# One core, five stages: attention's second scores of four heads in one block, routers with one exponential per step, counts in four pieces and list work shared anew

## The chip, the core and the metric

The kernel runs on one core of a Trainium2 chip. Its time is the device time of one execution in microseconds (us). The core has TensorE (PE; its weight loads are listed as PEld), VectorE (DVE), ScalarE (ACT), GpSimd (POOL) and the queue engine SyncE (SP). SP, ACT and POOL can issue DMAs; 16 DMA engines carry them. Engines run side by side, each in its own program order, and wait for one another through semaphores.

## The reference, cut to what matters

The program is two layers on 4096 tokens (16 sequences of 256) of 256 numbers. Two of its parts are touched by the change.

```python
def _moe(x, gate_w, w_gate, w_up, w_down):
    logits = x2 @ gate_w.T
    probs = jax.nn.softmax(logits.astype(jnp.float32), axis=-1)
    top_w, top_i = jax.lax.top_k(probs, K)
    ...
    pos = jnp.sum(jnp.cumsum(onehot, axis=0) * onehot, axis=-1) - 1
    valid = pos < C
```

There are E = 64 experts, K = 8 for each token and C = 128 places in each expert. The mixture of experts runs twice. Its first half, the router, gives each token's softmax weights and, for each expert, the list of its first 128 tokens in token order.

```python
def _chunk_abc(q, k, v, s):
    z = jax.lax.cumlogsumexp(s, axis=2)
    ...
    _, okT = jax.lax.scan(step_k, hk0, (qT, kT, pT, gT))
    pvT = jax.nn.softmax(okT, axis=-1)
    ...
    _, ovT = jax.lax.scan(step_v, hv0, (pvT, vT, pT, gT))
```

The attention has 16 heads and 64 slots and runs once, between the two mixtures. In the kernel both recurrences are causal products of 256 x 256 per head: the first scores are k times q, the second are exp(s) times pz (the softmax over slots divided by the running sum of exp(s)).

## The kernel before, in words

The stages follow one another, each in a block of its own: router 1 (`moe_router`, tiles `r_`), experts 1 (`e_`), attention (`a_`), router 2, experts 2, closing (`f_`). The order of each engine is written out by hand.

**Router.** NJ = 8 steps `j` of four tiles of 128 tokens: tiles 2j and 2j+1 of the lower half of the tokens and the same two of the upper half. Per step: DVE takes moments (`moments_of(j + 2)`), POOL makes `rstd` and `shift`, ACT normalises into `row` (L289), PE turns `row` (L474), ACT copies to `lnT` (L298), PE scores against the gate (L484), DVE copies logits, finds the eight largest, the negative maximum `nm` (L395), and the chosen experts (`choose(j)`). ACT then takes four exponentials, one per tile, with their sums (L319), DVE the reciprocal, and ACT scales the four into `row` (L327, four instructions). PE turns the chosen mask (L502) and DVE runs a cumulative count over the half (`cum`, L418). After step 6 (`EARLY`) ACT writes the counts of the first 12 tiles of each half to DRAM, after step 7 the rest (L304). They come back into `local` with tile number on the partitions (L218): 8 DMAs for the early part, 8 for the rest. Then comes the list work. PE sums the counts of earlier tiles (L507), DVE and POOL add them to `local`, half each (L430, L368), DVE marks which tile holds each slot (`reached` L433, `holds` L438), PE picks that tile's counts in 24 groups (L518) into six banks, and each group is counted in turn by DVE (even groups, L448) or ACT (odd groups, `Sign`, L342). The result, `slot_tok` (L462), is what the experts gather by.

**Attention.** N = 64 units `n` of four heads of one sequence. PE has a fixed order in which projections of unit n+1 (fp32r, `split_matmul`, L1432 to L1434) stand between the products of unit n. The second scores, `scores_b`, use two banks `psB`, one per head; heads are 64 rows deep (L1250, L1251), even heads on rows 0 to 63 and odd on 64 to 127. DVE masks each into `at` (L1081, `masked`). Because there are two banks, heads 0 and 1 go first, then `gate(n + 1, 0)`, then heads 2 and 3, then `gate(n + 1, 1)`, then `over_j`. `psD` (two banks) holds the turned output of unit n-1 until DVE has taken the low part of it (`low_of_output`, L1061, semaphore `otl_ok`), and then the result of `over_j(n)`.

Of the kernel before, what the change touches and what calls it, by code (L numbers as in the profile page):

```python
# [6 lines left out]

# [9 lines left out]
ALU = mybir.AluOpType  # L17
# [120 lines left out]
def moe_router(nc, cst, tag, past, x_src, gate_w, rows, fresh, slot_tok, counts):  # L138
# [6 lines left out]
    EARLY = 6  # L145
# [3 lines left out]
    with ExitStack() as ctx:  # L149
# [15 lines left out]
        nm = mem.sb("nm", [P, 2, 4])  # L165
        left = mem.sb("left", [P, 2, 2, E])
        chosen = mem.sb("chosen", [P, 2, 2, E])
        ex = mem.sb("ex", [P, 2, 2, 2, E])
# [24 lines left out]
        top, nm_ok, exps, rden_ok, weights = (mem.sem(n) for n in ("top", "nm_ok", "exps", "rden_ok", "weights"))  # L193
# [3 lines left out]
        cum_out = mem.sem2("cum_out")  # L197
# [3 lines left out]
        by_half = counts.rearrange("(e h r) -> h e r", h=2, r=HALF * P)  # L201
        by_tile = counts.rearrange("(g f h r t) -> f h r g t", f=4, h=2, r=HALF, t=P)
# [11 lines left out]
        def count_back(engine, parts, r0, r1):  # L214

            for f, h in parts:
                at = 32 * f + HALF * h
                engine.dma_start(local[at + r0:at + r1, :, 0:P], by_tile[f, h, r0:r1]).then_inc(local_here, 16)  # L218

        xv = x_src.rearrange("(h j p) d -> j p h d", h=2, p=P)  # L220
        rv = rows[0:NTOK, :].rearrange("(h j p) d -> j p h d", h=2, p=P)
        if fresh:
            stream_a, stream_b = fresh
            av = stream_a[0:NTOK, :].rearrange("(h j p) d -> j p h d", h=2, p=P)
            zv = stream_b.rearrange("(p k r) d -> p k (r d)", p=P, k=NZ)
        QUARTERS = [(f, h) for f in range(4) for h in range(2)]

        with nc.Block(no_gpsimd_drain=True) as block:  # L228
            @block.sync
            def _(sp):  # L230
# [14 lines left out]
                def rows_written(j):  # L245
                    sp.wait_ge(weights, 4 * j + 4)
                    for u in range(2):
                        sp.dma_start(rv[2 * j + u], row[:, j % R, u, :, :]).then_inc(row_out[j % R], 16)
# [5 lines left out]
                if fresh:  # L254
# [3 lines left out]
                    for k in range(NZ):  # L258
                        sp.dma_start(zv[:, k, :], zeros[:, :]).then_inc(zero_out, 16)
                for j in range(NJ - 1):  # L260
# [8 lines left out]
                rows_written(NJ - 1)  # L269
                sp.wait_ge(cum_out[1], 32)  # L270
                count_back(sp, QUARTERS[0:4], 2 * EARLY, HALF)
                if fresh:
                    for j in range(NJ - R, NJ):
# [8 lines left out]
            def _(act):  # L282
# [17 lines left out]
                def counts_out(r0, r1):  # L300
                    for u in range(2):
                        act.wait_ge(keyed[u], r1 // 2)
                    for h in range(2):
                        act.dma_start(by_half[h][:, r0 * P:r1 * P], cum[h * E:(h + 1) * E, r0 * P:r1 * P]).then_inc(cum_out[r0 > 0], 16)  # L304

# [5 lines left out]
                for j in range(NJ):  # L311
                    if j + 1 < NJ:
                        turned_out(j + 1)
                    act.wait_ge(nm_ok, j + 1)
                    if j >= 2:
                        act.wait_ge(weights, 4 * (j - 1))
                    for u in range(2):
                        for h in range(2):
                            nc.scalar.activation(ex[:, j % 2, u, h, :], lg[:, j % 2, u, h, :], ACT.Exp,  # L319
                                                 bias=nm[:, j % 2, 2 * u + h:2 * u + h + 1],  # L320
                                                 accum_out=den[:, j % 2, 2 * u + h:2 * u + h + 1]).then_inc(exps, 1)
                    if j + 2 < NJ:
                        normalise(j + 2)
                    act.wait_ge(rden_ok, j + 1)
                    for u in range(2):
                        for h in range(2):
                            nc.scalar.activation(row[:, j % R, u, h, D:ROW], ex[:, j % 2, u, h, :], ACT.Copy,  # L327
# [1724 lines left out]
```

## Time and profile before

| what | us |
|---|---|
| median of 3 runs (lowest, highest) | 2782.9 (2782.44, 2787.22) |
| the profiled execution's own time | 2797.33 |
| its span, first to last instruction | 2795.6 |
| PE busy | 2432.8 (87%) |
| DVE busy | 1789.0 (64%) |
| ACT busy | 888.8 (32%) |
| POOL busy | 1238.2 (44%) |

A view by windows gives busy time of each engine in a stretch, the TensorE clock that was granted (1.00 is 2.4 GHz, 0.50 is 1.2 GHz), the busy share of the 16 DMA engines and what they moved. Router 1 lies between 7 and 117 us of the span, experts 1 until about 375, attention until 1907, router 2 until 2018, experts 2 until about 2240, and the closing stage takes the rest.

### The profile page before, as it was taken

What the parts mean: (1) busy time and instruction counts of PE and PEld (TensorE: products, weight loads), DVE (VectorE), ACT (ScalarE), POOL (GpSimd) and SP (SyncE); (2) the same over time, 40 slices, a digit from 0 to 9 for tenths busy, and PEclk for the clock granted to TensorE, in tenths of its full rate; (3) what the DMA queues carried; (4) which work ended last, traced back from release to release, by engine and by line L of the source; (5) the groups of instructions that cost most, each with busy time, mean ns of one, the idle gap of its engine ahead of it and who ended that gap; (6) DMA issues with size and microseconds to landing.
All of it is one profiled execution on the core that took longest, in us unless ns stands there. A gap on an engine that the chain in (4) does not pass through costs nothing. (4 is left out here: it accounts for less than half of the span.)

```text
span 2795.6 us, 44639 instructions
## 1 busy us (share of the span) xinstructions
PE 2432.8 (87%) x16926; PEld 2117.8 (76%) x16926; DVE 1789.0 (64%) x3524; ACT 888.8 (32%) x1886; POOL 1238.2 (44%) x1200
## 2 busy tenths in 40 slices
PE   6465669999999999999999999996466578999997
PEld 5354458888888888888888888885455457888886
DVE  5332348877887787777777777774422247767654
ACT  6322223333333333333333333324422123333332
POOL 2277725454555455545544554542168712222110
PEclk9578889999999999999999999995588889999999
DMA  6698810000000000000000000003499710000000
GB/s 217 173 257 214 191 31 5 16 20 10 15 16 20 5 20 16 20 5 20 16 20 5 17 19 20 5 8 94 108 271 217 165 55 18 29 23 24 9 16 16
DMA packets 193219, 169.53 MB, mean 61 GB/s; under 512 B 28816, under 2 KB 185456, under 8 KB 192496
## 3 DMA queue, kind: packets, MB, share of 16 engines
q1 hardware_dynamic: 163776, 117.12, 14.2%
q0 software_dynamic: 24576, 37.77, 7.3%
q10 hardware_dynamic: 4656, 11.80, 1.4%
q8 instruction: 137, 2.24, 0.3%
q14 instruction: 74, 0.61, 0.1%
HBM read 117.94 MB, written 53.13 MB: 61 GB/s over the span
## 5 line engine op out<-in xcount | busy, mean ns | idle before, releaser
L1081 DVE TENSOR_TENSOR a_at<-a_psB,causal 128x384 f32<-128x384 f32 x512 | 260.6, 550 | 115.3 <-PE a_psB L1251 115.2
L948 POOL TENSOR_TENSOR a_orstd<-a_ms,minus_half 128x8 f32<-128x8 f32 x64 | 106.7, 1668 | 511.3 <-DVE a_ms L1108 510.0
L928 POOL TENSOR_SCALAR a_pick<-a_index,lut_row 128x258 f32<-128x258 int32 x240 | 279.9, 1166 | 24.3
L1101 DVE RECIPROCAL a_rz<-a_rz 128x256 f32<-128x256 f32 x128 | 215.6, 1716 | 0.0
L635 PE MATMUL e_psX<-ident,e_xg 128*128 128x128 f32 x256 | 64.5, 341 | 164.6 <-DMA e_xg<-rows,slot_tok 164.4
L759 DVE TENSOR_TENSOR e_hT<-e_psH,e_sil 128x128 f32<-128x128 f32 x128 | 37.3, 291 | 261.6 <-ACT e_sil L716 261.6
L635 PEld LDWEIGHTS e_psX<-ident,e_xg 128*128 128x128 f32 x256 | 33.3, 164 | 209.0 <-DMA e_xg<-rows,slot_tok 203.8
L931 POOL TENSOR_TENSOR a_found<-a_found,a_pick 128x258 f32<-128x258 f32 x240 | 177.5, 739 | 20.1
L1312 PEld LDWEIGHTS a_psD<-a_v,a_at 128*128 128x128 f32 x1536 | 181.3, 192 | 5.6
L1312 PE MATMUL a_psD<-a_v,a_at 128*128 128x128 f32 x1536 | 181.9, 275 | 0.0
L605 POOL DMA_INDIRECT e_xg<-rows,slot_tok x128 | 128.9, 1007 | 81.5 <-POOLq L228 43.1
L959 ACT ACTIVATE a_v<-a_psA 128x512 f32<-128x512 f32 x128 | 76.6, 598 | 246.6 <-PE a_psA L1434 246.6
L1432 PE MATMUL a_psC<-wo_high,a_oT 128*128 128x256 f32 x512 | 151.7, 296 | 1.5 <-DVE a_oT L1061 1.5
L1432 PE MATMUL f_pair<-f_lnT,wguT 128*128 128x512 f32 (+1 forms) x352 | 143.1, 406 | 7.5 <-DVE f_lnT L1698 7.2
L1433 PE MATMUL a_psC<-wo_low,a_oT 128*128 128x256 f32 x512 | 144.5, 282 | 0.0
L1434 PE MATMUL a_psC<-wo_high,a_oT 128*128 128x256 f32 x512 | 144.3, 282 | 0.0
L1433 PE MATMUL f_pair<-f_lnT,wguT 128*128 128x512 f32 (+1 forms) x352 | 140.4, 399 | 0.0
L1434 PE MATMUL f_pair<-f_lnT,wguT 128*128 128x512 f32 (+1 forms) x352 | 140.2, 398 | 0.0
L1709 DVE TENSOR_TENSOR f_hs<-f_pair,f_sil 128x512 f32<-128x512 f32 x96 | 66.1, 689 | 115.7 <-PE f_pair L1434 105.6
L953 POOL TENSOR_TENSOR a_o<-a_o,a_orstd 128x512 f32<-128x512 f32 x128 | 130.9, 1044 | 5.0
L1031 ACT ACTIVATE a_sq<-a_psD 128x512 f32<-128x512 f32 x128 | 76.5, 598 | 171.6 <-PE a_psD L1312 127.2
L959 ACT ACTIVATE a_emT<-a_psC 128x512 f32<-128x512 f32 x64 | 38.2, 597 | 283.5 <-DVE a_rz L1097 283.5
(248 smaller groups left out, 7532.0 us busy)
## 6 DMA issues: line engine op xcount, KB each, us to landing
e_wg<-in_L_ffn_w_gate SPq DMA_DIRECT2D x128, 128.0 KB, 3.5
e_wu<-in_L_ffn_w_up SPq DMA_DIRECT2D x128, 128.0 KB, 3.8
e_wd<-in_L_ffn_w_down SPq DMA_DIRECT2D x128, 128.0 KB, 4.3
rows<-r_row SPq DMA_DIRECT2D x32, 320.0 KB, 3.2
stream_b<-r_zeros SPq DMA_DIRECT2D x11, 384.0 KB, 6.0
stream_c<-rows SPq DMA_DIRECT2D x33, 128.0 KB, 3.2
r_xt<-in_L_attn_hidden_states SPq DMA_DIRECT2D x16, 256.0 KB, 3.9
stream_a<-r_xt SPq DMA_DIRECT2D x16, 256.0 KB, 5.2
```

The lines of the kernel that those rows point to most:

```text
L605: pool.indirect_dma_start(out=xg[:, e % U, :], out_offset=None, in_=rows, in_offset=bass.IndirectOffsetOnAxis(ap=slot_tok[:, e:e + 1], axi ...
L928: nc.gpsimd.tensor_scalar(pick[:, :, :], index[:, :, :], float(c), w["lut"][:, c:c + 1], ALU.is_equal, ALU.mult).then_inc(picked, 1)
L931: nc.gpsimd.tensor_tensor(out=found[:, :, :], in0=found[:, :, :], in1=pick[:, :, :], op=ALU.add).then_inc(looked, 1)
L948: nc.gpsimd.tensor_tensor(out=flat(orstd[:, :, :]), in0=ms[:, :], in1=cst["minus_half"][:, 0:TT * HQ], op=ALU.pow).then_inc(orstd_ok, 1)
L953: nc.gpsimd.tensor_tensor(out=part, in0=part, in1=orstd[:, :, 2 * a:2 * a + 2].unsqueeze(3).to_broadcast([P, TT, 2, DV]), op=ALU.mult).the ...
L959: nc.scalar.activation(out, in_, ACT.Copy, scale=scale).then_inc(done, 1)
L1081: nc.vector.tensor_tensor(out=at[:, h, :], in0=psB[h % 2][:, 0:3 * P], in1=cst["causal"][:, :, :].rearrange("p a i -> p (a i)"), op=ALU.mu ...
L1101: nc.vector.reciprocal(rz[:, a, :], rz[:, a, :]).then_inc(rz_ok, 1)
L1312: mm = nc.tensor.matmul(psD[:, t, h * DV:(h + 1) * DV], bt[:, h, i * P:(i + 1) * P], v[:, n % 2, j, h * DV:(h + 1) * DV], start=(j == 0), ...
L1432: nc.tensor.matmul(out, lhs[0], rhs[0], start=first, stop=False)
L1433: nc.tensor.matmul(out, lhs[0], rhs[1], start=False, stop=False)
L1434: return nc.tensor.matmul(out, lhs[1], rhs[0], start=False, stop=last)
```

## The change

The second scores of all four heads are issued in one block, heads 2 and 3 into the banks of `psD`; `over_j` waits for all four masks at once. In the routers, a step covers four tiles that follow one another in token order; DVE subtracts the maximum from all four tiles in one instruction (`below`), ACT takes one exponential of 256, DVE sums and inverts it, and POOL scales it into `row` (`weigh`). The counts go out in four pieces, three issued by SP in the course of the steps, and come back in four. In the list work ACT adds the counts of earlier tiles (16 instructions) and takes 9 of the 24 groups; DVE takes 15. In router 1, six of the eleven zero writes stand behind the counts' return on SP.

```diff
-        xv = x_src.rearrange("(h j p) d -> j p h d", h=2, p=P)
+        xv = x_src.rearrange("(j h p) d -> j p h d", h=2, p=P)
-        by_half = counts.rearrange("(e h r) -> h e r", h=2, r=HALF * P)
+        by_half = counts.rearrange("(e r h t) -> h e r t", r=HALF, h=2, t=P)
...
+        def by_sign(k):
+            return k % 4 == 3 or (k % 4 == 1 and k // 4 < len(TRIPLES) // 2)
+        def counts_out(engine, piece):
+            for u in range(2):
+                engine.wait_ge(keyed[u], STEP // 2 * (piece + 1))
+            r = slice(STEP * piece, STEP * (piece + 1))
+            for h in range(2):
+                engine.dma_start(by_half[h][:, r, :], cum[h * E:(h + 1) * E, r.start * P:r.stop * P].rearrange("e (r t) -> e r t", t=P)
+                                 ).then_inc(cum_out[piece], 16)
+        def count_back(engine, piece, quarters):
+            engine.wait_ge(cum_out[piece], 32)
+            k = slice(2 * STEP * piece, 2 * STEP * (piece + 1))
+            for f in quarters:
+                engine.dma_start(local[32 * f + k.start:32 * f + k.stop, :, 0:P], by_tile[f, k]).then_inc(local_here, 16)
...
-                    if j == EARLY:
-                        sp.wait_ge(cum_out[0], 32)
-                        count_back(sp, QUARTERS, 0, 2 * EARLY)
+                    piece, second = divmod(j, 2)
+                    if second and piece < NP - 1:
+                        counts_out(sp, piece)
+                    if not second and piece > 0:
+                        count_back(sp, piece - 1, range(4))
+                count_back(sp, NP - 1, (0, 1))
...
-                            nc.scalar.activation(ex[:, j % 2, u, h, :], lg[:, j % 2, u, h, :], ACT.Exp,
+                    nc.scalar.activation(ex[:, j % 2, :, :], below[:, j % 2, :, :], ACT.Exp).then_inc(exps, 1)
...
-                            nc.scalar.activation(row[:, j % R, u, h, D:ROW], ex[:, j % 2, u, h, :], ACT.Copy,
...
+                counts_out(act, NP - 1)
+                count_back(act, NP - 1, (2, 3))
+                act.wait_ge(passed_ok, 1)
+                act.wait_ge(local_here, 16 * 4 * NP)
+                for g in range(NG):
+                    nc.scalar.activation(local[:, g, 0:P], local[:, g, 0:P], ACT.Identity, bias=local[:, g, P + 1:P + 2]).then_inc(spread, 1)
...
-                    nc.vector.tensor_scalar(nm[:, j % 2, :], mx[:, j % 2, :, 0], -1.0, None, ALU.mult).then_inc(nm_ok, 1)
+                    nc.vector.tensor_tensor(out=below[:, j % 2, :, :], in0=lg[:, j % 2, :, :, :].rearrange("p u h e -> p (u h) e"),
+                                            in1=mx[:, j % 2, :, 0].unsqueeze(2).to_broadcast([P, 4, E]), op=ALU.subtract).then_inc(below_ok, 1)
...
+                    nc.vector.reduce_sum(den[:, j % 2, :], ex[:, j % 2, :, :], axis=AX.X).then_inc(den_ok, 1)
...
+                def weigh(j):
+                    pool.wait_ge(rden_ok, j + 1)
+                    nc.gpsimd.tensor_tensor(out=row[:, j % R, :, :, :].rearrange("p u h c -> p (u h) c")[:, :, D:ROW], in0=ex[:, j % 2, :, :],
+                                            in1=rden[:, j % 2, :].unsqueeze(2).to_broadcast([P, 4, E]), op=ALU.mult).then_inc(weights, 1)
...
-                def scores_b(n, heads):
+                def scores_b(n):
                     pe.wait_ge(pzt_ok, n + 1)
                     pe.wait_ge(et_ok, n + 1)
-                    for h in heads:
+                    for h in range(HQ):
                         if h < 2:
                             pe.wait_ge(at_ok, HQ * n + h + 3)
-                        else:
-                            pe.wait_ge(bt_ok, HQ * n + h - 1)
-                        causal_scores(emT, pzT, h, bt_ps)
+                        elif n > 0:
+                            pe.wait_ge(otl_ok, NH * n)
+                        causal_scores(emT, pzT, h, bt_ps, psO)
```

On PE, the place in attention is a unit in which `turn_stream` also stands; `psB0`, `psB1` and `psD` are banks, `wg` the gate's weights. Before:

```order
L1250 MATMUL a_psB0<-a_pzT,a_emT 128x256
L1251 MATMUL a_psB0<-a_pzT,a_emT 128x128
L1250 MATMUL a_psB1<-a_pzT,a_emT 128x256
L1251 MATMUL a_psB1<-a_pzT,a_emT 128x128
L1432 MATMUL a_psA0<-wg_high,a_lnT 128x512
...
L1187 MATMUL a_psC0<-ident,a_xab 128x128 x4
L1250 MATMUL a_psB0<-a_pzT,a_emT 128x256
L1251 MATMUL a_psB0<-a_pzT,a_emT 128x128
L1250 MATMUL a_psB1<-a_pzT,a_emT 128x256
L1251 MATMUL a_psB1<-a_pzT,a_emT 128x128
L1432 MATMUL a_psA1<-wg_high,a_lnT 128x512
```

The same place in the changed kernel (L1268 and L1269 are the former L1250 and L1251, L1449 the former L1432):

```order
L1268 MATMUL a_psB0<-a_pzT,a_emT 128x256
L1269 MATMUL a_psB0<-a_pzT,a_emT 128x128
L1268 MATMUL a_psB1<-a_pzT,a_emT 128x256
L1269 MATMUL a_psB1<-a_pzT,a_emT 128x128
L1268 MATMUL a_psD<-a_pzT,a_emT 128x256
L1269 MATMUL a_psD<-a_pzT,a_emT 128x128
L1268 MATMUL a_psD<-a_pzT,a_emT 128x256
L1269 MATMUL a_psD<-a_pzT,a_emT 128x128
L1449 MATMUL a_psA0<-wg_high,a_lnT 128x512
...
L1204 MATMUL a_psC0<-ident,a_xab 128x128 x4
L1449 MATMUL a_psA1<-wg_high,a_lnT 128x512
```

The four score instructions of heads 2 and 3 moved ahead of the first half of the gate; the number of instructions is the same.

On SP, router 1 from the last load of `r_xt` to the end of the router. Before:

```order
L238 DMA r_xt<-in_L_attn_hidden_states 128x2x256 x2
L248 DMA rows<-r_row 128x2x320 x6
L218 DMA r_local<-counts 12x16x128 x8
L248 DMA rows<-r_row 128x2x320 x2
L218 DMA r_local<-counts 4x16x128 x4
L243 DMA stream_a<-r_xt 128x2x256 x8
```

The changed kernel, the same stretch (L230 writes counts, L238 now reads them back, L293 writes zeros):

```order
L257 DMA r_xt<-in_L_attn_hidden_states 128x2x256 x2
L230 DMA counts<-r_cum 64x4x128 x2
L267 DMA rows<-r_row 128x2x320 x2
L238 DMA r_local<-counts 8x16x128 x4
L267 DMA rows<-r_row 128x2x320 x2
L230 DMA counts<-r_cum 64x4x128 x2
L267 DMA rows<-r_row 128x2x320 x2
L238 DMA r_local<-counts 8x16x128 x4
L267 DMA rows<-r_row 128x2x320 x2
L238 DMA r_local<-counts 8x16x128 x2
L293 DMA stream_b<-r_zeros 128x768 x6
L262 DMA stream_a<-r_xt 128x2x256 x8
```

Behind the last `rows` only two reads are left on SP (and two on ACT), where there were 8 ahead of it and 4 behind it.

## Rows read from the trace of the kernel before

**Rows 1.** The page's first line

```profile
span 2795.6 us, 44639 instructions
```

**Rows 2.** Windows: length, busy time (x instructions) of PE, PEld, DVE, ACT, POOL, clock, DMA, GB/s

```profile
387.00:1890.00 1503.00, 1496.69 (x11712) 1317.48 (x11713) 1186.88 (x1884) 481.16 (x836) 745.32 (x738) 1.00 0.05 14
1920.00:1976.60 56.60, 46.41 (x208) 39.57 (x208) 35.04 (x208) 41.97 (x142) 11.35 (x26) 0.53 0.39 121
1976.60:1994.20 17.60, 0.15 (x1) 0.15 (x1) 0.01 (x1) 0.49 (x3) 0.00 (x0) 0.50 0.70 153
```

**Rows 3.** Timeline of PE in router 1: start, us, engine, line

```profile
42.80 2.10 PE L474 MATMUL r_bank<-ident,r_row 128*128 128x128 f32 x8 [1.50 <-ACT r_row L289]
45.22 3.67 PE L484 MATMUL r_bank<-r_gwT,r_lnT 128*128 128x64 f32 x16 [0.32 <-ACT r_lnT L298]
...
59.48 3.68 PE L484 MATMUL r_bank<-r_gwT,r_lnT 128*128 128x64 f32 x16 [0.32 <-ACT r_lnT L298]
...
65.73 2.00 PE L484 MATMUL r_bank<-r_gwT,r_lnT 128*128 128x64 f32 x16 [0.32 <-ACT r_lnT L298]
```

**Rows 4.** Timeline of ACT in the same step

```profile
41.66 2.07 ACT L289 ACTIVATE r_row<-r_xt,r_shift,r_rstd 128x256 f32<-128x256 f32 x4 [2.71 <-POOL r_shift L364]
43.64 1.05 ACT L327 ACTIVATE r_row<-r_ex,r_rden 128x64 f32<-128x64 f32 x4
44.59 1.05 ACT L298 ACTIVATE r_lnT<-r_bank 128x512 f32<-128x512 f32 x2
```

**Rows 5.** Timeline of DVE in the same step

```profile
42.78 0.17 DVE L395 TENSOR_SCALAR r_nm<-r_mx 128x4 f32<-128x4 f32 x1
...
43.64 0.48 DVE L404 TENSOR_TENSOR r_chosen<-r_left,r_lg 128x128 f32<-128x128 f32 x2
```

**Rows 6.** The counts' trip in router 1: DMA view, landing times, timeline, windows

```profile
counts<-r_cum ACTq DMA_DIRECT2D x2, 128.0 KB, 3.3
...
DMA to landing us min/median/max: 3.3/3.9/6.8
...
79.61 4.59 SPq L218 DMA_DIRECT2D r_local<-counts  x4
...
92.27 0.61 PE L507 MATMUL r_psG<-r_local,earlier 128*128 128x16 f32 x2 [20.85 <-DMA r_local<-counts]
...
82.00:84.00 2.00, 0.00 (x0) 0.00 (x0) 0.00 (x0) 0.00 (x0) 0.00 (x0) 0.50 0.95 91
```

**Rows 7.** Timeline of DVE, list work of router 1

```profile
93.14 0.19 DVE L425 TENSOR_TENSOR r_passed<-r_local 128x16 f32<-128x16 f32 x1
...
94.50 2.92 DVE L433 TENSOR_TENSOR r_reached<-slot_row,r_local 128x1024 f32<-128x1024 f32 x1
97.45 2.19 DVE L438 SCALAR_TENSOR_TENSOR r_holds<-slot_row,r_passed,r_reached 128x128 f32<-128x128 f32 x8
99.56 1.22 DVE L433 TENSOR_TENSOR r_reached<-slot_row,r_local 128x1024 f32<-128x1024 f32 x1
...
116.32 0.23 DVE L462 TENSOR_TENSOR slot_tok<-r_tok,r_fill 128x64 uint32<-128x64 f32 x1
```

**Rows 8.** Timeline of PE, attention

```profile
1002.85 1.53 PE L1284 MATMUL a_psC<-a_at,a_em 128*64 128x128 f32 x24
...
1012.03 0.28 PE L1433 MATMUL a_psA<-a_lnT,wk_high 128*128 128x256 f32 x1
1012.15 0.28 PE L1434 MATMUL a_psA<-a_lnT,wk_low 128*128 128x256 f32 x1
1012.36 0.71 PE L1250 MATMUL a_psB<-a_pzT,a_emT 64*128 64x256 f32 x4
...
1013.22 0.50 PE L1432 MATMUL a_psA<-wg_high,a_lnT 128*128 128x512 f32 x1
1013.56 0.40 PE L1433 MATMUL a_psA<-wg_low,a_lnT 128*128 128x512 f32 x1
```

**Rows 9.** Timeline of DVE, the same unit

```profile
1011.25 1.29 DVE L1061 TENSOR_TENSOR a_oT<-a_psD,a_oT 128x512 fp32r<-128x512 f32 x2
```

More of the change, by code:

```diff
@@ L196, in moe_router @@
             mem.sem(n) for n in ("local_here", "base_set", "lo_ps", "lo_ok", "passed_ok"))
-        cum_out = mem.sem2("cum_out")
+        cum_out = [mem.sem(f"cum_out{k}") for k in range(NP)]
         spread, reached_ok, holds_ok = (mem.sem(n) for n in ("spread", "reached_ok", "holds_ok"))
@@ L212, in of_bank, with rank @@
             return table.rearrange("p (g f) -> p g f", f=4)[:, first:first + n, e4]
[L214 to L218, printed above, removed]
-        xv = x_src.rearrange("(h j p) d -> j p h d", h=2, p=P)
-        rv = rows[0:NTOK, :].rearrange("(h j p) d -> j p h d", h=2, p=P)
+        def by_sign(k):
+            return k % 4 == 3 or (k % 4 == 1 and k // 4 < len(TRIPLES) // 2)
+        def rank(k):
+            return sum(by_sign(i) == by_sign(k) for i in range(k))
+        def counts_out(engine, piece):
[11 more added lines that the diff above has]
+        xv = x_src.rearrange("(j h p) d -> j p h d", h=2, p=P)
+        rv = rows[0:NTOK, :].rearrange("(j h p) d -> j p h d", h=2, p=P)
         if fresh:
             stream_a, stream_b = fresh
-            av = stream_a[0:NTOK, :].rearrange("(h j p) d -> j p h d", h=2, p=P)
+            av = stream_a[0:NTOK, :].rearrange("(j h p) d -> j p h d", h=2, p=P)
             zv = stream_b.rearrange("(p k r) d -> p k (r d)", p=P, k=NZ)
-        QUARTERS = [(f, h) for f in range(4) for h in range(2)]
         with nc.Block(no_gpsimd_drain=True) as block:
@@ L245, in rows_written @@
                 def rows_written(j):
-                    sp.wait_ge(weights, 4 * j + 4)
+                    sp.wait_ge(weights, j + 1)
                     for u in range(2):
@@ L313, in _ @@
                         turned_out(j + 1)
-                    act.wait_ge(nm_ok, j + 1)
+                    act.wait_ge(below_ok, j + 1)
                     if j >= 2:
-                        act.wait_ge(weights, 4 * (j - 1))
-                    for u in range(2):
-                        for h in range(2):
-                            nc.scalar.activation(ex[:, j % 2, u, h, :], lg[:, j % 2, u, h, :], ACT.Exp,
-                                                 bias=nm[:, j % 2, 2 * u + h:2 * u + h + 1],
-                                                 accum_out=den[:, j % 2, 2 * u + h:2 * u + h + 1]).then_inc(exps, 1)
+                        act.wait_ge(weights, j - 1)
@@ L351, in _, with scales @@
                 nc.gpsimd.tensor_copy(local[:, :, P], cst["tile_base"][:, 0:1].to_broadcast([P, NG])).then_inc(base_set, 1)
-                for j in range(NJ):
+                def scales(j):
                     k = j % 2
@@ L834, in attention @@
         psD = mem.ps("psD", [P, 2, 512])
+        psO = [psD[:, k, :] for k in range(2)]
         names = ("x_here x_out_done xs_ok xacc_ok stats moments shifted rstd_ok ln_ok ln_ps lnTh_ok lnTl_ok "
```

119 lines of the change are left out of this document (54 added, 65 removed).

## The prediction

> **What bounds the kernel now.** I read the span first [rows 1], then the busy time by stages [rows 2]. In attention, 1503.0 us long, PE is busy for 1496.7 us at a granted clock of 1.00, and it hardly waits: whatever time goes from PE's own sequence there goes from the kernel. The routers are different. In router 2 the eight steps take 56.6 us with PE busy for 46.4 at a clock of 0.53, then 17.6 us pass in which no engine computes [rows 2]; in router 1 PE waits 20.85 us at this place, for the counts that come back from DRAM [rows 6]. So I went to the timelines: of PE, ACT and DVE for the steps [rows 3 to 5], of the queues for the trip of the counts [rows 6], of DVE for the list work [rows 7]. Nothing of the next stage can start before `slot_tok` is there, so each microsecond of a router counts in full.
>
> **Attention.** The work stays and one interruption goes. A pair of heads takes PE from 1012.36 to 1013.22, 0.86 us [rows 8]. How much of it is work? A head is 384 columns, each instruction issued in two parts, so a pair gives each half of the array 768 columns. L1284 issues 24 parts of 128 columns over two halves, 1536 for each half, exactly what four heads would be, and lasts 1.53 us with its tail; to the next start I take 1.50 [rows 8]. So 768 columns more cost 0.64 us, and 0.22 of the pair's 0.86 is filling and emptying. That halves do run side by side is seen in the pair too: the four L1250 that begin at 1012.36 last 0.71 in all [rows 8]. Four heads in one block then take 1.50 us where two pairs took 1.72. Around a pair the steps of the projections stretch too: 0.21 from 1012.15 to 1012.36 where 0.12 is usual (1012.03 to 1012.15), and the first L1432 behind it lasts 0.50 against 0.40 [rows 8]; 0.09 + 0.10 = 0.19 us for each pair that stands alone. One such edge goes. Sum per unit: 0.22 + 0.19 = **0.41 us**, in 63 of 64 units (the last has no projections between): **25.8 us**. The low end is the edge alone, 63 x 0.19 = 12 us, if the two pairs don't flow into one another. I see nothing that could give more.
>
> The Trainium skill weighs in here against the change: "TensorE: Matmul & The Clock Gate", Part 3, says that matmuls begin and end strictly in program order. By that, heads would overlap only where one ends and the next begins, a pair would be about 1.28 us and some filling, and a block of four would gain the edge alone, 12 us. The row's 0.86 us for a pair does not agree, so I keep 25.8.
>
> The new waits: head 2 now waits for `otl_ok`, the low part of the turned output, since it writes over it. DVE ends that at 1012.54 [rows 9] in a unit in which it also normalises the stream; PE reaches head 2 some 0.64 us after 1012.36, at 1013.0. That leaves 0.47 us, so the cost is nothing; without this cover each 0.1 us costs 6.3 us in all. `over_j` waits for all four masks: four masks of about 0.49 us end near 1015.3, and PE comes there after both halves of the gate, at about 1017.2. DVE's scans wait behind two masks more, but it no longer waits for the second pair, and it ends its inverses earlier than now. POOL and ACT keep their work there.
>
> **The routers' steps.** The period of two steps is 59.48 - 45.22 = 14.26 us [rows 3]. It is a chain: choose, moments, `rstd` on POOL, normalise, turn, `lnT`, scores, mask, count, next choose. ACT is on it with L298: PE's first half of the turn is through at about 42.80 + 1.15 = 43.95, but ACT is scaling weights from 43.64 and copies only at 44.59 [rows 3, 4]. These four go to POOL, so 0.6 us come off. DVE's `nm` (0.17 us, of which 0.07 hold the next back) becomes a subtraction of 256 columns; two of 128 take 0.48 [rows 5], so I take 0.34, and 0.27 more on the chain. Net -0.33 for each crossing, three crossings: **-1.0 us per router**. The sum `den` and the reciprocal stand where DVE waits for the mask anyway; the four exponentials that become one were not on the chain. `weigh` on POOL comes behind `scales(j + 2)`, where POOL has some 5 us free; a product of 256 there is under 1 us and only `rows` on SP waits for it.
>
> POOL and DVE can hold each other up. L433 took 2.92 us while POOL's half of the addition ran, and 1.22 without [rows 7]. If each `weigh` blocked DVE on the chain for 0.8 us, it would cost 4 x 0.8 = 3.2 us per router instead of nothing. I take nothing, since `weigh` falls on DVE's wait for the mask or its reads of PSUM. The Trainium skill, "SBUF — State Buffer", calls it an exclusive lock between the two engines and holds it for the whole instruction; by that rule the worst case is the same 3.2.
>
> **The counts' trip.** Three quarters of it move into the steps. Behind the last count the changed kernel issues two writes (1.0 us), waits until they land, issues two reads on each of two queues (1.0 us), and waits. Packets are 512 B: in 82 to 84, where such reads alone ran, 91 GB/s at a share of 0.95 make 16 x 0.95 x 512 / 91 = 85 ns each [rows 6], so 512 packets over 16 engines 2.7 us. A write of that size landed in 3.3 us with larger packets, and counts' landings range to 6.8 [rows 6]; I take 4.6. For the reads the upper end is 84.20 to 92.27, 8.1 us with the backlog of the early reads, the lower 3.3; I take 5.0. Trip: 1.0 + 4.6 + 1.0 + 5.0 = **11.6 us** (8.6 to 16.9). Router 2: 17.6 - 11.6 = **6.0 us** gained. Router 1: the 20.85 include 1.3 for the last count, so 19.55 - 11.6 = **8.0**. On SP the new wait for each piece holds up `keep`, `rows` and the next load; the load is needed two steps (14 us) later, so it is covered, and would cost up to 3 us per piece if not. The six zero writes move behind the reads and lie under the list work (20 us; they and the kept rows are 4.3 MB).
>
> **The list work.** From L425's end at 93.33 to `slot_tok` at 116.55 it takes 23.2 us [rows 7]. DVE loses its half of the addition, and L433 its block. What is left is DVE in a row: 2 x 1.22, 2 x 2.19, and 40 experts at 2.19 / 8 = 0.27 plus 15 small copies at 0.1 (12.3), then 1.2 for the end: 20.3 us. ACT's 16 additions (0.34 each by the 128x256 and 128x64 forms, 0.5 and 0.26 [rows 4], so 5.4) end before DVE's `holds`, and PE, at the lower clock, has 14 us of picks. **-2.8 us per router** (0 to -4.5).
>
> **Sum.** Routers 1.0 + 8.0 + 2.8 and 1.0 + 6.0 + 2.8 = 21.6; attention 25.8; together 47.4. From the profiled execution's own 2797.3 (span 2795.6 [rows 1]) to 2749.9; that execution stood 14.4 above the median of the runs, so against 2782.9 it is **2735.5 us**.
>
> **The rivals.**
> - The edge alone in attention: 12 instead of 25.8 gives 2749. For it stands that a wait lies between heads 1 and 2; against it the pair's 0.86.
> - The clock rises early in a router. All scores took 3.67 us but the last, which took 2.00 [rows 3]; in router 2 the steps' clock is 0.53 and the same last one was fast, so nearly all of them run at 1.2 GHz. PE's gaps get shorter. Once up, a crossing loses 1.7 us of scores and some 0.6 of the rest, up to 7 us per router; I price it at 10 for both: 2725.
> - The trip stays long, at 16.9: 5.3 more in each router, 2746; with POOL's lock in both, 2752.
> - Attention doesn't gain at all, as PE's gaps were the sequencer's own: 2761.
> - Slower: `otl_ok` comes late. PE stalls in each unit by what DVE's L1061 ends later than 0.47 us from now. It decides from 0.47 + 47.4 / 63 = 1.22 us late; at 1.5 us the kernel takes 2735.5 + 63 x 1.03 = 2800. DVE is behind PE nowhere in that stretch now, which speaks against it.
>
> **How the numbers follow.** Forecast 60%; edge alone 13%; early clock 14%; long trip 8%; no gain in attention 2%; slower 3%. Within the forecast the time lies between 2727 and 2746. The range that leaves out 2 in 10 or less takes in the early clock and the edge alone: 2718 to 2755. A measurement of this kernel tells 0.2%, 5.6 us, from no change. All cases but the last lie below that: faster 0.96, same 0.01, slower 0.03.
>
> **What would show it.** In the changed kernel's timeline: L1268 and L1269 take 1.5 us in one stretch, with no wait between; a unit is 0.41 us shorter; PE stays at a clock of 1.00 and idle for a few us only in attention. In the routers PE waits for counts for 12 to 13 us; `reached` lasts 1.22 both times; the steps take 1 us less. It is wrong if PE waits for `a_oT` in attention, or if the reads of the last piece land after 8 us.

## The result, and the profile after

Timed beside each other on one chip, the changed kernel took 2757.1 us (median of 4 runs, 2750.6 to 2762.1) and the kernel before 2785.1 (4 runs): ratio 0.9897, 95% interval 0.987 to 0.9925, 28 us less. Two later groups gave 2754.5 against 2791.0 (0.9865, 0.9848 to 0.9883) and 2748.6 against 2787.3 (0.9863, 0.9844 to 0.9881), 36 and 39 us less. In the first of these one slow execution of the kernel before, 5046.7 us, is left out. The change is faster, by less than the 47 us forecast. The first time lies 2 us above the range and 22 above the forecast; the two later ones lie inside the range, at 19 and 13 above the forecast.

The profiled execution, 2760.5 us long, is set against the rows of before. The page's first line [rows 1]:

```profile
span 2758.7 us, 44491 instructions
```

The windows of attention, of router 2's steps and of its trip [rows 2], with the same columns:

```profile
401.90:1863.40 1461.50, 1454.71 (x11556) 1304.64 (x11552) 1177.25 (x1858) 477.21 (x825) 746.59 (x738) 1.00 0.05 14
1888.00:1945.60 57.60, 47.30 (x208) 41.27 (x208) 40.69 (x220) 28.24 (x56) 16.02 (x36) 0.50 0.53 147
1945.60:1957.10 11.50, 0.61 (x2) 0.50 (x2) 0.48 (x3) 0.00 (x0) 0.50 (x1) 0.50 0.49 110
```

The first window runs from the first `a_ms` to the last (DVE, once a unit), the measure of attention used below; in the first profile of before it is 1482.3 us. Attention is still PE's, at a clock of 1.00. The trip's windows, 17.6 and 11.5 us, do not begin and end at the same marks; from the end of the last cumulated count to PE's first use of what came back, router 2 takes 17.4 us in before and 10.4 now.

PE's timeline in attention [rows 8] shows where the forecast was too high:

```profile
1015.78 0.28 PE L1451 MATMUL a_psA<-a_lnT,wk_low 128*128 128x256 f32 x1
1015.99 0.71 PE L1268 MATMUL a_psB<-a_pzT,a_emT 64*128 64x256 f32 x4
1016.53 0.39 PE L1269 MATMUL a_psB<-a_pzT,a_emT 64*128 64x128 f32 x4
1016.75 0.70 PE L1268 MATMUL a_psD<-a_pzT,a_emT 64*128 64x256 f32 x4
1017.18 0.49 PE L1269 MATMUL a_psD<-a_pzT,a_emT 64*128 64x128 f32 x4
1017.60 0.50 PE L1449 MATMUL a_psA<-wg_high,a_lnT 128*128 128x512 f32 x1
```

From its start to the start of the next instruction (L1449) the block takes 1017.60 - 1015.99 = 1.61 us, not 1.50. Its first pair takes 0.76 and the second 0.85. There is no idle time between them. The forecast's 1.50 was read off L1284 of before, which begins at 1002.85 [rows 8]. The row behind it is this one:

```profile
1004.31 0.39 PE L1432 MATMUL a_psA<-ws_high,a_lnT 128*128 128x256 f32 x1
```

So L1284 takes 1.46 us from start to start for the same 1536 columns per half. But its rows name the part of the array that an instruction uses 128*64, and the scores' rows name theirs 64*128: the price was borrowed from another form. DVE in the same unit as the block [rows 9]:

```profile
1014.88 1.29 DVE L1079 TENSOR_TENSOR a_oT<-a_psD,a_oT 128x512 fp32r<-128x512 f32 x2 [0.73 <-ACT a_oT L977]
1016.95 1.02 DVE L1100 TENSOR_TENSOR a_at<-a_psB,causal 128x384 f32<-128x384 f32 x2 [0.78 <-PE a_psB L1269]
1017.89 1.01 DVE L1100 TENSOR_TENSOR a_at<-a_psD,causal 128x384 f32<-128x384 f32 x2
```

`otl_ok` comes at 1016.17, 0.58 us before PE reaches head 2 (0.47 was forecast). In router 1, PE's steps [rows 3]:

```profile
42.84 2.10 PE L491 MATMUL r_bank<-ident,r_row 128*128 128x128 f32 x8 [1.77 <-ACT r_row L310]
44.73 3.58 PE L501 MATMUL r_bank<-r_gwT,r_lnT 128*128 128x64 f32 x16
...
58.65 3.59 PE L501 MATMUL r_bank<-r_gwT,r_lnT 128*128 128x64 f32 x16
...
64.90 3.58 PE L501 MATMUL r_bank<-r_gwT,r_lnT 128*128 128x64 f32 x16
```

Two steps take 58.65 - 44.73 = 13.92 us instead of 14.26, and the 0.32 us that PE waited for `lnT` are gone. The last score stays at 3.58, where it had fallen to 2.00 in this profile of before. The trip [rows 6], in the timelines of ACT, SP and PE:

```profile
73.24 1.33 ACTq L230 DMA_DIRECT2D counts<-r_cum  x2
78.08 0.95 ACTq L238 DMA_DIRECT2D r_local<-counts  x2
...
73.26 0.89 SPq L267 DMA_DIRECT2D rows<-r_row  x2
78.07 0.66 SPq L238 DMA_DIRECT2D r_local<-counts  x2
...
83.62 0.61 PE L524 MATMUL r_psG<-r_local,earlier 128*128 128x16 f32 x2 [11.08 <-DMA r_local<-counts]
```

From the first write's issue to PE it is 83.62 - 73.24 = 10.4 us: 1.3 of issue, 3.5 until the write has landed, 1.0 of issue, 4.6 until the reads have. DVE's list work [rows 7]:

```profile
84.49 0.19 DVE L444 TENSOR_TENSOR r_passed<-r_local 128x16 f32<-128x16 f32 x1
84.71 1.22 DVE L448 TENSOR_TENSOR r_reached<-slot_row,r_local 128x1024 f32<-128x1024 f32 x1
85.97 2.19 DVE L453 SCALAR_TENSOR_TENSOR r_holds<-slot_row,r_passed,r_reached 128x128 f32<-128x128 f32 x8
88.08 1.22 DVE L448 TENSOR_TENSOR r_reached<-slot_row,r_local 128x1024 f32<-128x1024 f32 x1
...
104.88 0.23 DVE L479 TENSOR_TENSOR slot_tok<-r_tok,r_fill 128x64 uint32<-128x64 f32 x1
```

L448 takes 1.22 us both times, and from the end of `passed` (84.68) to the end of `slot_tok` (105.11) are 20.4 us, where 20.3 was forecast.

### The profile page after: what moved, and what is told of

Same layout as the page of the kernel before. It is cut to its first block and busy times, and to the rows that moved or that the text cites. A ratio compares the mean times of both kernels' runs of the same rounds, so it can differ in the third digit from the quotient of the medians.

```text
span 2758.7 us, 44491 instructions
## 1 busy us (share of the span) xinstructions
PE 2413.2 (87%) x16926; PEld 2123.4 (77%) x16926; DVE 1805.3 (65%) x3578; ACT 864.9 (31%) x1704; POOL 1245.1 (45%) x1214
## 5 line engine op out<-in xcount | busy, mean ns | idle before, releaser
L1100 DVE TENSOR_TENSOR a_at<-a_psB,causal 128x384 f32<-128x384 f32 x384 | 195.5, 551 | 58.6 <-PE a_psB L1269 58.6
L1449 PE MATMUL a_psC<-wo_high,a_oT 128*128 128x256 f32 x512 | 151.9, 297 | 1.5 <-DVE a_oT L1079 1.5
L1449 PE MATMUL f_pair<-f_lnT,wguT 128*128 128x512 f32 (+1 forms) x352 | 143.6, 408 | 7.5 <-DVE f_lnT L1715 7.2
L717 ACT ACTIVATE e_xgT<-e_psX 128x256 f32<-128x256 f32 x128 | 49.1, 384 | 243.2 <-PE e_psX L652 199.2
```

The costliest lines, as they stand in the source:

```text
L1100: nc.vector.tensor_tensor(out=at[:, h, :], in0=bank[:, 0:3 * P], in1=cst["causal"][:, :, :].rearrange("p a i -> p (a i)"), op=ALU.mult).th ...
L1449: nc.tensor.matmul(out, lhs[0], rhs[0], start=first, stop=False)
```

## The experiments

Stage times are starts of the same instructions in each profile: "to the counts", from the span's start to DVE's first copy of `psG`; "list", from there to `slot_tok`; "experts 1", to the last issue of the gathered rows' write; "attention", as above; "steps and trip 2", from the last `a_ms` to the second router's copy of `psG`.

**The kernel before again, the change again, and its two halves.** `e_attn` is the kernel before with the hunks of attention, `e_router` with those of the router.

> The kernel before, unchanged, for a second profile of it. The question is where its first profile (2797.3 us, some 12 us over the other runs) was long. Theory A, the extra time lay in one stage: this profile stands near 2785 and one stage is 10 us or more shorter than in the first (attention 1503, or the experts 240.3 and 215.8, or the closing stage 551.0). Rival, runs differ by a little everywhere: each stage differs by its share, 1 to 6 us in attention and the closing stage. In either case the routers' waits (20.85 us before the first list, 17.6 in the second router) should repeat within 1.5 us.

> The changed kernel, unchanged, timed over five rounds. By the first comparison of the profiles the gain by terms is 11.4 in router 1, 9.3 in router 2, 20.8 in attention, less 1.4 and 2.5 given back in the experts and 1.0 in the closing stage, in all 36.6 us; by the medians it is 28. If the terms are real and the first profile of the kernel before was long only by chance in stages that the change does not touch, the median of this one stands 30 to 37 us below before (ratio 0.987 to 0.989). If attention gains less than the profiles say, it stands near 28 again (0.990).

> Only the attention part of the change: four heads of second scores in one block, in a kernel whose routers are those of before. Theory A, the terms add up and the block of four takes 1.61 us: 18 to 22 us faster than before (ratio about 0.993), with the block at 1.61 and no wait of PE in it. Rival, attention gains the edge alone: 12 us. Rival, the block would be 1.50 as predicted and the routers' part disturbs it: 26 us.

> Only the routers' part: one exponential, the counts in four pieces, list work shared anew, with the attention of before. Theory A, the routers gain 11.4 and 9.3 by the profiles and the experts behind them give back 1.4 and 2.5: 15 to 18 us faster in all (ratio about 0.994). Rival, nothing is given back: 20.7. Rival, the experts and the closing stage are bound by transfers that the routers' earlier end only makes wait longer: 8 to 12. What e_attn and this one gain should add up to what the whole change gains, within 3 us.

```
run            time us     to counts  list  experts 1  attention  steps+trip 2
before         2785-2791      92.9    23.4    240.3     1482.3      100.2
before_again   2785.6         89.3    23.4    233.6     1480.2      100.0
e_attn         2768.5         88.0    23.4    235.9     1460.9       98.8
e_router       2776.2         83.8    20.6    238.0     1481.9       93.4
after          2757.1         84.3    20.6    241.7     1461.5       93.7
after_again    2754.5         84.3    20.6    239.9     1462.3       93.8
```

`e_attn` gains 22.4 us on the medians (ratio 0.992, 0.990 to 0.9941), `e_router` 14.7 (0.9945, 0.9929 to 0.996): 37.2, where the whole change gains 36.5 beside them. Within the scatter of the runs the halves add up and do not disturb each other. Attention gains 19.9 us on the means of three profiles with each form of it; the edge alone (12) and the 26 are out. Two stages scatter. The first experts take 231.4 to 245.4 us over the seventeen profiles of this study, so the 1.4 us that seemed given back in the first two profiles were chance. And the time to the counts differs between three profiles of one and the same router, since PE's wait in the chain of waits does. In `before_again`:

```profile
PE r_psG L507 <- DMA r_local<-counts: 16.2, 1, 16.2
```

and in `e_attn`:

```profile
PE r_psG L507 <- DMA r_local<-counts: 14.2, 1, 14.2
```

against 20.9 in the profile on which the forecast rests [rows 6]. The changed kernel's is 10.5 to 11.2 in three profiles.

**The waits of the block.** A rival for the missing 0.11 us: the wait for `otl_ok` between heads 1 and 2.

```diff
+                    pe.wait_ge(at_ok, HQ * n + 4)
+                    if n > 0:
+                        pe.wait_ge(otl_ok, NH * n)
                     for h in range(HQ):
-                        if h < 2:
-                            pe.wait_ge(at_ok, HQ * n + h + 3)
-                        elif n > 0:
-                            pe.wait_ge(otl_ok, NH * n)
```

> The changed kernel, unchanged, as the measure for the other three kernels of this group: about 2755 us. Its stages should repeat those of the first two profiles: 84.3 us to the first counts, 20.6 of list work, 240 in the first experts, 1462 in attention (first to last moments), 93.7 from there to the second counts.

> The changed kernel with the waits of the block of four heads (for the masks and for the turned output's low part) all ahead of its first head, so that nothing stands between heads 1 and 2. The block takes 1.61 us where 1.50 was forecast; its second half starts 0.76 us after the first where work alone would be 0.64. Theory A, the wait between heads 1 and 2, though long satisfied, costs the 0.12: the block falls to 1.50, attention to 1455 us (7 less). Rival, the 0.12 is what switching to another bank, or the start of a second pair of heads, costs by itself: block 1.61, attention unchanged at 1462. Rival, the turned output's low part comes later than the block now starts: PE waits for it and attention is longer.

The unchanged copy (`after_third`) took 2748.6 us, `e_waits` 2774.6: it gives back more than attention had gained (1485.5 us, copy 1460.8). PE's timeline in it:

```profile
1020.67 0.28 PE L1450 MATMUL a_psA<-a_lnT,wk_low 128*128 128x256 f32 x1
1021.20 0.71 PE L1268 MATMUL a_psB<-a_pzT,a_emT 64*128 64x256 f32 x4 [0.25 <-DVE a_oT L1079]
1021.71 0.42 PE L1269 MATMUL a_psB<-a_pzT,a_emT 64*128 64x128 f32 x4
1021.93 0.70 PE L1268 MATMUL a_psD<-a_pzT,a_emT 64*128 64x256 f32 x4
1022.36 0.49 PE L1269 MATMUL a_psD<-a_pzT,a_emT 64*128 64x128 f32 x4
1022.78 0.49 PE L1448 MATMUL a_psA<-wg_high,a_lnT 128*128 128x512 f32 x1
```

The block still takes 1.58 us with no wait in it, and the second pair again 0.85: the wait between the heads was not the cause. But ahead of the block the same wait is now open in 63 units, for 0.24 to 0.39 us in 61 of them (0.25 in this one) and for 2.0 and 1.5 in two, 19.7 us in all. As PE stands still behind the projections, 1021.20 - 1020.67 = 0.53 us pass where 0.21 did. That is the rival "slower", reached by a placement instead of a late DVE. Attention is 24.7 us longer. Four units in a row take 94.33 us instead of 93.11, so a usual unit costs 0.30, which makes 19 us; most of the rest lies in the unit with the wait of 2.0 us and in the last one (20.6 instead of 17.5).

**The zeros, and five pieces.** Two doubts on the router. `e_zeros` sets `ZFIRST = 11`; `e_pieces` cuts the counts at 0, 4, 8, 12, 14, 16 tile columns instead of 0, 4, 8, 12, 16.

> The changed kernel with all eleven writes of zeros issued at the start, as before, instead of six of them behind the reads of the last counts. The experts of the first router took 233.6 to 240.3 us with the routers of before and 238.0 to 241.7 with the changed ones. Theory A, the six late writes fall on the list work and the first gathers and delay them: the first experts' stage falls by about 3 us to 237, and the counts' trip is not longer, since the early zeros are out before. Rival, the experts' stage varies by itself: it stays between 234 and 242, and the early zeros delay the loads of the first steps or the pieces of counts, as before: time to the first counts above 84.3 by 1 to 4 us.

> The changed kernel with the counts in five pieces, the last two of two tile columns each instead of one of four, so that half as much is written and read behind the last count (256 packets of 512 B instead of 512). Theory A, the trip is two latencies and packets at 85 ns each over 16 engines: 1.35 us less in the reads and some tenths in the write, so the counts come 1.5 to 2 us earlier in each router, 3 to 4 us in all. Rival, latency and issue alone make the trip: no difference. Rival, the reads of the fourth piece, issued one step later now, are still under way and delay the last ones: 1 us slower.

`e_zeros` took 2752.3 us (0.987, 0.9851 to 0.989) and has the unchanged copy's stages: 83.5 to the counts (83.4), experts 1 232.3 (231.4). When the zeros go out makes no difference that these profiles show. `e_pieces` took 2750.4 (0.9869, 0.9848 to 0.9889); steps and trip 2 are 94.9 instead of 93.3. From the end of the last cumulated count to PE's first use it is 10.77 and 11.35 us in the two routers, where the unchanged copy has 9.84 and 10.41. Half as many packets in the last piece brought nothing, and the trip is 0.9 us longer, as the rival had it.

**A pair's price, and the order of the heads.** `e_extra` computes heads 0 and 1 twice; `e_order` has `for h in (0, 1, 3, 2)`.

```diff
+                    for g in (0, 1):
+                        r = slice(g * DK, g * DK + DK)
+                        nc.tensor.matmul(psB[g][:, 0:2 * P], emT[r, 0, 0:P], pzT[r, 0, 0:T], start=True, stop=True)
+                        nc.tensor.matmul(psB[g][:, 2 * P:3 * P], emT[r, 0, P:T], pzT[r, 0, P:T], start=True, stop=True)
                     for h in range(HQ):
```

> The changed kernel with heads 0, 1, 3, 2 in the block of second scores instead of 0, 1, 2, 3 (and the masks in that order). In the traces the two halves of the array begin the second pair together, but then one half runs 0.11 us behind the other, and the block takes 1.61 us where 1.50 was forecast. A wait between heads 1 and 2 is not the cause: with all waits ahead of the block it still lagged. Theory A, the lag belongs to the order in which the parts of the second pair are handed to the halves: with head 3 first it goes or moves, and attention is up to 0.11 us a unit shorter, 1455 us instead of 1461. Rival, each pair behind another one loses the same whatever the order: 1461 us.

> The changed kernel with the scores of heads 0 and 1 computed twice in the block of second scores, so that three pairs follow one another (the outputs are the same). It measures the price of a pair inside a block. Theory A, a pair in a block costs its 768 columns a half, 0.64 us, and the lag of 0.11 comes once: block 2.25 us, attention 1461 + 63 x 0.64 = 1501 us. Rival, every pair behind another one pays the lag: 0.75 us each, attention 1508. If halves did not run side by side at all, it would be 1.28 more: 1541. The forecast of 0.64 us for a pair is right in the first case only.

`e_extra` (2792.2 us; attention 1502.4, expected 1501 and 1508) in PE's timeline:

```profile
1024.90 0.71 PE L1290 MATMUL a_psB<-a_pzT,a_emT 64*128 64x256 f32 x4
...
1025.66 0.70 PE L1268 MATMUL a_psB<-a_pzT,a_emT 64*128 64x256 f32 x4
...
1026.32 0.70 PE L1268 MATMUL a_psD<-a_pzT,a_emT 64*128 64x256 f32 x4
...
1027.17 0.50 PE L1454 MATMUL a_psA<-wg_high,a_lnT 128*128 128x512 f32 x1
```

The pairs take 0.76, 0.66 and 0.85. A pair in the middle costs 0.66 us, in the stage's length (1502.4 - 1461.5) / 63 = 0.65: the forecast's 0.64 stands. Beside 0.64 for the work, the first pair pays 0.12 and the last some 0.2; a pair alone pays 0.22 in all (0.86). So a block saves 2 x 0.86 - 1.61 = 0.11 of the 0.22, not all of it. In `e_extra` the first two pairs both write `psB`, and the first still takes 0.76, so going on to another bank is not the cause. `e_order` took 2749.9 us, attention 1461.5: the order of the halves is not it either. What in the second pair makes the block end 0.1 us later stays open.

**The rows out of the trip's way.** Two writes of 320 KB, the last step's rows, were issued on SP beside the counts' last writes (the expectation counts one of the two).

```diff
-                    rows_written(j)
+                    if j < NJ - 1:
+                        rows_written(j)
...
                 count_back(sp, NP - 1, (0, 1))
+                rows_written(NJ - 1)
```

> The changed kernel with the last step's rows (320 KB) written behind the reads of the last counts instead of between their write and their reads. The last piece's write lands in 3.9 us where the same piece, written during the steps, lands in 2.8 to 3.0. Theory A, the rows' packets stand in the way of the counts' write: the trip of the counts is 0.5 to 1 us shorter in each router (10.5 us from the last cumulated count to the first use in router 2 instead of 11.4). Rival, the trip is latency alone: no difference. Rival, the rows then delay the reads: 0.5 us longer.

It took 2749.6 us (0.9849, 0.9832 to 0.9865). No unchanged copy ran beside it, and `e_order`, which did and has the rows' writes in their old place, took 2749.9, so the time itself shows no gain; the stages do. The timelines of ACT and PE in router 1:

```profile
73.14 1.33 ACTq L230 DMA_DIRECT2D counts<-r_cum  x2
76.35 0.96 ACTq L238 DMA_DIRECT2D r_local<-counts  x2
...
81.82 0.61 PE L526 MATMUL r_psG<-r_local,earlier 128*128 128x16 f32 x2 [9.37 <-DMA r_local<-counts]
```

The reads start 3.2 us behind the write instead of 4.8, and the trip is 81.82 - 73.14 = 8.7 us instead of 10.4. Steps and trip 2 fall from 93.7 to 92.0.

**The first scores in one block too.** `e_join` makes the change's own edit once more: `psD` is free from the gated output's read to the next turned output.

```diff
+                        elif m > 0:
+                            pe.wait_ge(o1_ok, TT * m)
+                            pe.wait_ge(sq_ok, TT * m)
-                        causal_scores(kT, qT, h, at_ps)
+                        causal_scores(kT, qT, h, at_ps, psO)
...
-                    if ahead:
-                        scores_a(n + 1, (0, 1))
                     if n > 0:
                         output(n - 1)
                     if ahead:
-                        scores_a(n + 1, (2, 3))
+                        scores_a(n + 1, range(HQ))
```

DVE's masks follow in the same way, all four behind `add_output`.

> The changed kernel with the same edit made to the first scores: heads 2 and 3 go to the banks of the output, which are free once the gated output and the squares have read them, so the first scores of four heads stand in one block behind the output projection, and DVE masks all four there. Theory A, what a second isolated pair costs (0.11 us of filling and emptying and 0.21 of edge, 0.325 us a unit as measured) is saved again: attention 1461 - 62 x 0.325 = 1441 us. Rival, the masks now come late: DVE has four masks (2 us) behind the addition of the output before the squares, and PE waits for them in the read of the slots; attention stays at 1461 or is longer.

2730.2 us (0.9788, 0.9771 to 0.9804), attention 1441.2 as expected by theory A. PE's timeline:

```profile
1008.73 0.28 PE L1447 MATMUL a_psC<-wo_high,a_oT 128*128 128x256 f32 x1
1008.94 0.71 PE L1266 MATMUL a_psB<-a_qT,a_kT 64*128 64x256 f32 x4
...
1009.70 0.70 PE L1266 MATMUL a_psD<-a_qT,a_kT 64*128 64x256 f32 x4
...
1010.55 0.49 PE L1445 MATMUL a_psA<-wv_high,a_lnT 128*128 128x512 f32 x1
```

Again 1.61 us for the block, and PE doesn't wait in this unit: DVE masks until 1011.93, and PE's read of the slots starts at 1012.14, so the cover is 0.2 us for the last mask and more for the first. Four units in a row fall from 93.11 to 91.93 us, 0.29 a unit, which makes 18 of the 20.3 us; the rest lies at the stage's two ends. Behind the stage, steps and trip 2 are 94.8 us instead of 93.7, so about 1 us of it is given back there.

**Sums, and the trip of before.** `e_best` has both edits, `e_best5` the five pieces as well. `e_early4` is the kernel before with `EARLY = 4`.

> The changed kernel with both edits that gained: the first scores of four heads in one block too, and the last step's rows behind the reads of the counts. If they add up: attention 1441 us, from the last cumulated count to its first use in router 2 9.8 us, in router 1 82.5 us to the counts; in time 2730.2 less 1.5 and 1.1, about 2727 us (ratio 0.977 to 0.978). Rival, the rows now hold up the zeros and the kept rows behind them and the list's stage ends later: 2730 or more.

> The same with the counts in five pieces, the last two half as large. Alone, five pieces made the trip 1 us longer (12.4 instead of 11.4), and the rows' writes stood between the write and the reads there. Theory A, the fourth piece's reads were late because of the rows and collided with the last piece's: with the rows out of the way the trip is 0.5 to 1.3 us shorter than with four pieces (9.8 in router 2). Rival, the fourth piece's reads can only start when its write has landed, 3 us before the last piece's own, and share its queues in any case: 0.5 to 1 us longer than 9.8.

> The kernel before with the counts cut at step 4 instead of 6: the first half goes out and comes back during the steps, the second half behind the last. Theory A, the reads of the first three quarters, issued 0.5 us after the last write, are the backlog in which the last reads wait, and make PE's wait for the counts long and uneven (20.9, 16.2, 14.2 us in three profiles): with them gone the wait in router 1 is about 1.3 + 1.3 of issue + 4.5 for a write of 256 KB + 1.3 + 6.5 for reads of 1024 packets = 15 us, and in router 2 about the same. Rival, the backlog is nothing and the last part's own size sets the wait: 20 us or more, as twice as many packets are read behind the last count.

`e_best` took 2725.3 us (0.978, 0.9763 to 0.9798), 63.7 below before and the fastest here: attention 1440.6, 81.9 to the counts, steps and trip 2 93.0. From the end of the last cumulated count to PE's first use it is 8.2 and 8.5 us in the two routers. `e_best5` took 2735.0 (0.9806): 84.8 to the counts, and 11.2 and 11.9 us for that trip. So with the rows out of the way the five pieces cost 3 us in each router instead of 1: the rows' place was not what spoiled them. `e_early4` took 2781.5 (0.9983, 0.9967 to 0.9998), although twice as much is written and read behind the last count. Its chain of waits in router 1:

```profile
PE r_psG L507 <- DMA r_local<-counts: 14.0, 1, 14.0
```

and 14.1 in router 2, where before has 18.0 and 18.2, and `e_attn`, with the same router, 13.9. So the reads of the first three quarters, issued right ahead of the last part's, can be the backlog that makes the trip long. It isn't shown: of the six routers in three profiles with these reads, four have waits of 16 to 21 us and two have 14 as well, and two routers of `e_early4` are few to tell a cure from chance.

## Why the prediction was wrong

The mechanisms that gave the terms of the sum were right. Three steps failed: the block of four heads was priced too low (1.50 us, measured 1.61), the wait for the counts in the one profile of before was taken for the usual one, above all in router 1 (19.55 us from the last count, 16.3 in the mean of three profiles), and the sum was set against that same long profile. The sum was 47.4 us. The means of the table's three profiles with each form give 37.4: attention 19.9, to the counts 5.9, steps and trip 2 6.0, list work twice 2.8; what differs elsewhere is within its scatter. The first timing showed only 28 us of it, the two later ones 36 and 39. So of the 21.6 us between 2735.5 and 2757.1, 10 are the terms, 2 the median of before (2785.1 there, 2782.9 in the forecast) and 9 are scatter of that timing; in its profile the first experts took 241.7 us, in `after_third` 231.4.

- **Attention, -25.8: mis-sized, 19.9.** "0.22 of the pair's 0.86 is filling and emptying" was right, but the step from there, "four heads in one block then take 1.50 us", took all of it as saved. The block takes 1.61. The 1.50 came from L1284, whose rows have another form (128*64), and no row of a block of scores was there to test it. Four units in a row took 94.39 us and now take 93.11, 0.32 a unit: 0.11 for filling and 0.21 for the edge, where 0.22 and 0.19 were forecast; 63 times that is 20.2. The last unit gives back up to 1.0 of it (17.3 us before, 17.7 to 18.4 in the three profiles of the table with the block), which the forecast didn't see: with no projections left to cover them, `over_j` waits there for all four masks, 1.2 us in the profiled execution.
- **The Trainium skill's rule on this.** "TensorE: Matmul & The Clock Gate", Part 3, lets matmuls begin and end strictly in program order. That heads could by this overlap only where one ends and the next begins was my reading, and it was wrong: the same Part has matmuls in different row groups of the array run at the same time. One more pair costs 0.65 us here, where heads one behind another would cost 1.28, so the trace agrees with that, and the rival "the edge alone" fell.
- **`otl_ok` costs nothing: right where it stands, with 0.58 us to spare.** `e_waits` shows how near the other side was: 0.76 us earlier, at the block's head, the same wait is open.
- **The steps, -1.0 per router: right.** In router 1 two steps take 13.92 us (44.73 to 58.65) instead of 14.26 [rows 3], so three crossings give 1.0, and ACT's copy no longer holds PE.
- **The clock that rises early: it did not come; a fast score became rarer instead.** The steps' windows of router 2 have a granted clock of 0.53 in before and of 0.50, the lower level throughout, now. The last score took 2.00 us in both routers of before's profile and 3.58 now, so between these two profiles the end of the steps loses what the crossings gained. It isn't a fixed trait of either router: `e_attn`, with the router of before, has 0.50 too and a last score of 3.67 and 3.68 us. Over all profiles the last score was fast in 5 of 8 routers of the form of before and in 1 of 26 of the changed form; why is open. In that one, `e_order`'s router 1, four scores took 2.0 to 2.3 us. The last count ended at 70.80 us instead of 73.16, but its trip was 1.4 us longer (11.9), and the time to the counts is 83.3: an early clock gained 1 us at most, where the rival had 5 in a router.
- **The counts' trip, 11.6: 10.4, right within its bounds.** The gain in router 1, -8.0, was wrong: it was taken from a wait of 20.9 us, and the same router waits 16.2 and 14.2 in other profiles. Steps and trip together gain 5.9 in router 1 instead of 9.0, and 6.0 instead of 7.0 in router 2. Some luck hides how wrong the old trips were taken: from the end of the last count they are 16.3 and 16.1 us in the means of three profiles, not 19.55 and 17.6, and the new one, 1.2 us shorter than forecast, made up for part of that. In router 2 the last score, 2.00 us in two of the three profiles of before and 3.6 in all of the changed ones, explains the 1.0 that is missing.
- **The list work, -2.8 per router: right**, in every profile (23.4 to 20.6).
- **The offset.** The profiled execution of before stood 14.4 us above the median, and the sum was set against it as if that excess lay in nothing that the change touches. Beside `before_again` it was longer by 3.6 us to the counts, 6.7 in the first experts and 2.1 in attention: part of the excess was the very wait that was then counted as gain.
- **The range.** Its upper end took in the edge alone, but not a block that saves half its filling together with a shorter wait of before. These two, 5.9 and 3.1 us, are 9 of the 10 that the terms fell short by; by the terms alone the time would have been 2745.5, inside the range.

The Trainium skill's page "TensorEngine Tiling (Array Packing)", Key Properties, says that a change of tiling mode drains TensorE. The rows agree with a price for each stretch of 64-row instructions between 128-row ones: beyond 0.64 for each pair, a lone pair costs 0.22 us and 0.21 at its edge, and a block of two or of three pairs 0.33 or 0.34 and the same edge. A stretch that was merged with another gave 0.32 us a unit in the change and 0.29 in `e_join`. That the drain is this price is argued, not shown; no run takes the drain by itself.

## What to carry to other kernels

Instructions that use half the array's rows cost, in this kernel, their columns plus about 0.4 us for a lone pair between full ones and 0.55 for a block of two or three pairs, so two stretches merged save about 0.3; gather them into as few stretches as banks and waits allow, and look for a bank that is idle just then, as `psD` was. Put a wait at the instruction that needs it, not at the block's head: a wait of 0.25 us that PE had not met before cost 0.30 in each usual unit. Price a block by rows of the same form, or call the price a guess. And before a wait is booked as gain, see in more than one profile how long it is, the more so when the profiled execution stands above the median.

## What was not expected of the hardware

- A wait of 0.25 us ahead of the block was not hidden in the gap that is there anyway: that gap grew from 0.21 to 0.53 us, and the block behind it became only 0.03 shorter (1.58 instead of 1.61).
- Two writes of counts (128 KB each) beside two of rows (320 KB each) kept their readers waiting for 4.8 us from the first issue, and without the rows 3.2.
- With nothing changed in the router, PE's wait for the counts was 13.9 to 20.9 us in six routers of three profiles, and the first experts, the same in all seventeen profiles, took 231 to 245 us.
